# Where the ternary quantization of six weight matrices sits inside the context stage of a fused eight-layer kernel

## The reference, cut to what matters

```
# for each of the 8 context batches: what later attention layers need of the context
k = rms_norm(ctx @ wk_ctx);  v = ctx @ wv_ctx              # layer 1
kv = feature_map(ctx @ Wk)^T (ctx @ Wv)                    # layer 2 (linear attention)
k3, v3 = ctx @ wkv + bkv                                   # layer 3

# for each of six feed-forward weight matrices (gate, up, down of layers 0 and 1)
scale = mean(abs(w)) (+ or max 1e-5)
wq    = clip(round(w / scale), -1, 1) * scale              # so: -1, 0 or +1 times scale
```

## Time and profile before

| | us |
|---|---|
| median of three executions | 2215.29 |
| the profiled execution's own time | 2214.09 |
| its span in the trace | 2212.3 |
| TensorE busy | 2062.1 (93% of the span) |
| VectorE busy | 1121.0 (51%) |
| ScalarE busy | 826.5 (37%) |
| GpSimd busy | 181.4 (8%) |

### The profile page before, as it was taken

One profiled execution on the slowest core, in us unless ns is written; L12 is line 12 of the kernel. 1 busy time (PEld: TensorE's weight loads), 2 busy tenths in 40 slices (PEclk: granted clock), 3 DMA queues, 4 the chain that ended last, 5 costly groups with the idle time before them and its releaser, 6 DMA issues.

```text
span 2212.3 us, 28740 instructions
## 1 busy us (share of the span) xinstructions
PE 2062.1 (93%) x10661; PEld 1168.5 (53%) x10684; DVE 1121.0 (51%) x2469; ACT 826.5 (37%) x1717; POOL 181.4 (8%) x466
## 2 busy tenths in 40 slices
PE   8999999999999798999999999999488888888999
PEld 3444444444666344555555555566244445556665
DVE  1324554258121485555555555487355568774221
ACT  1232233321111264445444455355232235553331
POOL 0011110000000121101110110010100100000000
PEclk9999999999999999999999999999799989998999
DMA  5354442451641511120000011300100502220000
GB/s 227 130 209 174 163 155 103 193 207 60 212 138 59 196 57 42 38 89 21 22 22 22 22 29 40 135 18 10 37 16 15 177 29 88 81 64 10 11 11 15
DMA packets 60315, 185.13 MB, mean 84 GB/s; under 512 B 10578, under 2 KB 29010, under 8 KB 54463
## 3 DMA queue, kind: packets, MB, share of 16 engines
q1 hardware_dynamic: 58451, 145.55, 19.1%
q0 software_dynamic: 1728, 37.75, 4.4%
HBM read 124.61 MB, written 49.50 MB: 79 GB/s over the span
## 4 chain that ended last, share of the span: by engine, by line
PE 71%; DVE 15%; issue 5%; ACT 4%; DMA 2%; POOL 1%; SPq 1%; DVEq 0%; POOLq 0%; ACTq 0%
PE psum L120 47%; PE psum L113 8%; PE psum L1558 5%; PE psum L2612 4%; PE psum L1603 4%; DVE R L654 3%; ACT R L583 2%; DVE small L2491 2%; DVE R L653 1%; PE psum L1146 1%; DVE R L1313 1%; PE psum L2420 1%; DMA d_kv<-WK 1%; DVE R L1312 1%; DVE WK L2497 1%
## 5 line engine op out<-in xcount | busy, mean ns | idle before, releaser
L120 PE MATMUL psum<-R,WK 128*125 128x512 f32 (+10 forms) x3144 | 1084.3, 491 | 34.3 <-DMA WK<-in_ctxT 7.9
L120 PEld LDWEIGHTS psum<-R,WK 128*112 128x112 f32 (+4 forms) x3158 | 516.7, 172 | 545.3 <-issue 421.5
L113 PE MATMUL psum<-small,WK 112*125 112x112 f32 (+5 forms) x2036 | 286.3, 271 | 77.8 <-DVE WK L1303 20.1
L113 PEld LDWEIGHTS psum<-small,WK 112*125 112x125 f32 (+5 forms) x2036 | 225.0, 155 | 185.3 <-issue 76.6
L120 PE MATMUL psum<-WK,R 128*32 128x128 f32 (+5 forms) x1880 | 221.9, 354 | 25.6 <-DMA WK<-d_cd 12.0
L1734 DVE TENSOR_REDUCE small<-psum 112x1 f32<-112x487 f32 x128 | 85.1, 665 | 194.2 <-PE psum L120 190.3
L120 PEld LDWEIGHTS psum<-WK,R 128*32 128x32 f32 (+4 forms) x1880 | 120.2, 135 | 107.7 <-issue 46.8
L1558 PE MATMUL psum<-R,WK 128*112 128x512 f32 x256 | 120.1, 592 | 0.0
L1653 ACT ACTIVATE WK<-psum,small 112x487 f32<-112x487 f32 x128 | 96.9, 757 | 54.2 <-DVE small L1736 53.2
L1603 PE MATMUL psum<-R,WK 125*128 125x448 f32 (+1 forms) x256 | 107.6, 543 | 0.0
L1646 ACT ACTIVATE WK<-WK,small 112x487 f32<-112x487 f32 x128 | 90.0, 703 | 45.8 <-DVE small L1728 45.7
(11 more groups left out here) (237 smaller groups left out, 2137.6 us busy)
## 6 DMA issues: line engine op xcount, KB each, us to landing
R<-in_wf POOLq DMA_DIRECT2D x6, 4096.0 KB, 13.8
d_w<-R POOLq DMA_DIRECT2D x6, 2048.0 KB, 18.1
R<-d_w SPq DMA_DIRECT2D x6, 2048.0 KB, 11.1
WK<-in_ctxT SPq DMA_DIRECT2D x16, 750.0 KB, 6.7
d_v<-WK SPq DMA_DIRECT2D x16, 750.0 KB
R<-in_wq SPq DMA_DIRECT2D x7, 1024.0 KB, 8.0
R<-in_wo SPq DMA_DIRECT2D x6, 1024.0 KB, 15.0
d_k<-X SPq DMA_DIRECT2D x8, 750.0 KB, 5.2
```

The costliest lines, as they stand in the source:

```text
L113: ins = pe.transpose(dst, src, idn[0:k, 0:k])
L120: ins = pe.matmul(dst, lhs, rhs, start=k == 0, stop=k == len(pairs) - 1)
```

## The change

Four edits, all within `context_part`:

- ScalarE takes the four sums of absolute values one at a time, each behind the copy of `k3_0` to `k3_3` (and so ahead of the copy of `T_2`, and of `turn` and `spread` in batches 4 and 5). Each adds one to `context_abs`, and VectorE's sum waits for four of them.
- VectorE makes ternary matrix b no longer at the end of batch b, but behind `v3_0` of batch b + 1 (a function of its own, `ternary`).
- POOL's two transfers go with it: they stand behind the inverse root of sub-tile 0 of batch b + 1.
- SP waits for the last ternary store, and loads the spline inputs, behind the load of context batch 7 instead of ahead of it.

```diff
@@ sync @@
                     sp.dma_start(ctxT[:, b % 2], io.ctxT[:, b]).then_inc(sem(f"context_ctxT{b % 2}"), 16)
+                    if b == 7:
+                        sp.wait_ge(sem("context_ternary"), 6)
+                        sp.wait_ge(sem("ternary_stored"), 16 * 6)
+                        for dst, src in ((table[:, 0], io.table[0]), (table[:, 1], io.table[1]), (points, io.points),
+                                         (knot, io.knot), (way, io.way)):
+                            sp.dma_start(dst, src).then_inc(sem("spline_inputs"), 16)
                     store(sp, b - 1)
...
                     if b == 7:
                         stages[0]["load"](sp)
-                    if b == 6:
-                        sp.wait_ge(sem("context_ternary"), 6)
-                        sp.wait_ge(sem("ternary_stored"), 16 * 6)
-                        for dst, src in ((table[:, 0], io.table[0]), (table[:, 1], io.table[1]), (points, io.points),
-                                         (knot, io.knot), (way, io.way)):
-                            sp.dma_start(dst, src).then_inc(sem("spline_inputs"), 16)
@@ act @@
                         ins.then_inc(act_ring.sem_drained, 1)
+                        if kind == "k3" and b < 6:
+                            if j == 0:
+                                act.wait_ge(sem("context_raw"), 16 * (b + 1))
+                                if b:
+                                    act.wait_ge(sem("ternary_stored"), 16 * b)
+                            act.activation(tern[:, j * 2048:(j + 1) * 2048], raw[:, j * 2048:(j + 1) * 2048], ACT.Abs,
+                                           accum_out=wsum[:, b, j:j + 1]).then_inc(sem("context_abs"), 1)
...
-                    if b < 6:
-                        act.wait_ge(sem("context_raw"), 16 * (b + 1))
-                        if b:
-                            act.wait_ge(sem("ternary_stored"), 16 * b)
-                        for c in range(4):
-                            ins = act.activation(tern[:, c * 2048:(c + 1) * 2048], raw[:, c * 2048:(c + 1) * 2048],
-                                                 ACT.Abs, accum_out=wsum[:, b, c:c + 1])
-                        ins.then_inc(sem("context_abs"), 1)
@@ dve @@
+                        if s == 0 and 1 <= b <= 6:
+                            ternary(dve, link, b - 1)
                         if b == NB - 1:
...
                     if b < 6:
-                        dve.wait_ge(sem("context_abs"), b + 1)
+                        dve.wait_ge(sem("context_abs"), 4 * (b + 1))
...
-                        dve.wait_ge(sem("context_threshold"), b + 1)
-                        for cols in parts:
-                            under = below[:, 0:cols.stop - cols.start]
-                            link(dve.tensor_scalar(under, raw[:, cols], thr[:, b, 1:2], None, ALU.is_lt))
-                            ins = dve.scalar_tensor_tensor(tern[:, cols], raw[:, cols], thr[:, b, 0:1],
-                                                           under, ALU.is_gt, ALU.subtract)
-                            if cols.stop < WF:
-                                link(ins)
-                        ins.then_inc(sem("context_ternary"), 1)
...
+            def ternary(dve, link, w):
+
+                dve.wait_ge(sem("context_threshold"), w + 1)
+                for cols in parts:
+                    under = below[:, 0:cols.stop - cols.start]
+                    link(dve.tensor_scalar(under, raw[:, cols], thr[:, w, 1:2], None, ALU.is_lt))
+                    ins = dve.scalar_tensor_tensor(tern[:, cols], raw[:, cols], thr[:, w, 0:1], under, ALU.is_gt, ALU.subtract)
+                    if cols.stop < WF:
+                        link(ins)
+                ins.then_inc(sem("context_ternary"), 1)
@@ pool @@
                         pool.tensor_tensor(rk, ssp, neghalf[0:SP, :], ALU.pow).then_inc(sem("context_norms"), 1)
+                        if s == 0 and 1 <= b <= 6:
+                            pool.wait_ge(sem("context_ternary"), b)
+                            if b < 6:
+                                pool.dma_start(raw, io.wf[b]).then_inc(sem("context_raw"), 16)
+                            pool.dma_start(d_w[b - 1], tern).then_inc(sem("ternary_stored"), 16)
...
-                        pool.wait_ge(sem("context_ternary"), b + 1)
-                        if b + 1 < 6:
-                            pool.dma_start(raw, io.wf[b + 1]).then_inc(sem("context_raw"), 16)
-                        pool.dma_start(d_w[b], tern).then_inc(sem("ternary_stored"), 16)
```

## The result

| | before | changed | ratio, 95% interval |
|---|---|---|---|
| first comparison, median (executions) | 2212.03 us (7) | 2204.29 us (7) | 0.9957 [0.9943, 0.9971] |
| repeated with the experiments | 2211.43 us (19) | 2204.81 us (12) | 0.9975 [0.9962, 0.9988] |
| profiled execution: own time, span | 2214.09, 2212.3 us | 2204.48, 2202.7 us | |

The change makes the kernel faster, by 0.43% in one comparison and 0.25% in the other; the two intervals overlap only between 0.9962 and 0.9971. The ratios aren't the quotients of the medians; those are 0.9965 and 0.9970, which is 7.7 and 6.6 us. The forecast was 0.9968 as a ratio (2208.3 of 2215.3).

A forecast was written before the change was run, and what follows sets the result against it. TensorE, busy 93% of the span, was taken as the bound, losing time at `T_0` of batches 1 to 6. From 2214.1 us, -21.5 + 10.9 + 3.6 = -7.0 gave 2207.1, or 2208.3 against the median 2215.3; range 2203.5 to 2214.0.

The forecast's parts named there:

- Removal of the stalls, 21.5 us: TensorE's waits at `T_0` of batches 1 to 6, with second waits and slow clock behind them, all go: 21.5 us.
- the second wait of 0.52 us: Right behind each stall at `T_0` of batches 1 to 6, TensorE waits 0.52 us for ScalarE, which needs `kn` too.
- The new stall, 10.9 us: At the ends of batches 0 to 5, the copy of `T_2` stands behind the fourth sum, delaying TensorE: 10.9 us.
- The clock in the stage, two drops of 1.8 us: At two of the six new idle gaps TensorE's clock falls, costing 1.8 us each: 3.6 us, bounds 0 and 10.8.
- The stage's sum: Context stage: -21.5 for the stalls, +10.9 for the new stall, +3.6 for the clock, together -7.0 us.
- Its own time lies 1.2 under the median of 2215.3, against which the forecast is 2208.3: Whole kernel: the profiled execution's 2214.1 us less 7.0 gives 2207.1, restated against the median 2215.3 as 2208.3 us.
- Nothing behind the stage absorbs it: Behind the context stage: attention 0 starts from the last stores, which shift with batch 7, so the -7.0 us stays.
- No drops at all (1): At the new gaps between batches the clock never falls; 2204.7 us, chance 0.14.
- drops at four or more of the six places (2): The clock falls at four to six batch boundaries; 2211.9 to 2215.5 us, no change, chance 0.17.
- The late store (3): The ternary store lands too late for ScalarE's first sum, delaying batches; 2223.8 us at 25 us landing, chance 0.09.
- A stall in sub-tile 1 (4): `kn` of sub-tile 1 comes too late for `T_1`; 2215 us or so, no change, chance 0.05.

The follow-up runs named there:

- the second experiment: Against the changed kernel, only the fourth sum of absolute values moved behind ScalarE's copy of `T_2`; 2192.04 us, ratio 0.9913 to the kernel before.
- The fifth sum: Against the changed kernel, one more sum of absolute values put between the fourth and the copy of `T_2`; 2224.16 us, ratio 1.0057 to the kernel before.
- third experiment: Against the changed kernel, all four sums put back behind the copy of `T_2`, so only the ternary matrix and its transfers moved; 2191.14 us, ratio 0.9908.
- the last experiment: Against the kernel with only the ternary matrix moved, SP's wait for the last ternary store put back ahead of batch 7's load; 2192.57 us, ratio 0.9922.
- the sixth experiment: Against the changed kernel, POOL's two transfers put behind the inverse root of sub-tile 2 instead of 0; 2263.85 us, ratio 1.0244 to the kernel before.

## Why the prediction was right or wrong

**Removal of the stalls, 21.5 us: right.** TensorE no longer waits for `kn`, and in the kernel with the fourth sum behind `T_2` batches 1 to 6 take 389.2 us (75.29 to 464.45), for which 389.4 had been worked out as unstalled. One reading was off, without a part in the sum: the second wait of 0.52 us stands behind five of the six `T_0`, not behind that of batch 1.

**The new stall, 10.9 us: right in place, cause and size.** Forecast 1.8 us at four batch starts and 1.85 in batches 4 and 5. TensorE's waits are 1.82 and 1.96, and the delay is 1.89 at each of the six, which is one sum: from the last context product to the next batch it is 2.86 us (73.82 to 76.68) where the second experiment has 0.97 (266.50 to 267.47), and from `kv` to `spread` 3.19 (338.69 to 341.88) where it has 1.30 (330.03 to 331.33). Six of them are 11.3 us. The forecast was 0.4 short, and the fifth sum took 1.89 more at each.

**The clock in the stage, two drops of 1.8 us: right in the profiled execution.** Batch 1's group of 80 lost 1.7 us. At the end of batch 4, from `spread` to the next batch 3.26 us pass (341.88 to 345.14) instead of 2.62 (331.33 to 333.95), and the group behind takes 35.22 instead of 34.57: 1.3 us together. The repeat had three drops. In the four profiles with idle times of 1.82 us at batch starts (the changed kernel twice, only the sums moved, the transfers late) the clock fell behind 3 of 13 of them, in batch 1, 1 and 4, and behind 4 of the 6 waits of 1.96 us in the first three of these profiles. So the same idle time does not always have the same price. The spread of the executions points the same way, but isn't proof: in the second and third experiment, without idle time at the batch starts, they lie within 2189.3 to 2195.0 and 2189.9 to 2192.4, in the changed kernel's repeat within 2200.4 to 2210.7, and before within 2204.2 to 2216.3; the last experiment, also without such idle time, has one execution at 2199.8 beside five within 2189.9 to 2194.8.

**The stage's sum.** Six batches took 410.9 us before and take 389.2 without stalls, so -21.7; with 11.3 for the new stall, 3.0 for the two drops and -0.6 from the stage's start that is -8.0. Measured: -8.1. The forecast had -7.0 for the same stage; 0.6 of the difference is batch 0's transfers, 0.6 the smaller second drop, and -0.2 and +0.4 the two stalls.

**"Its own time lies 1.2 under the median of 2215.3, against which the forecast is 2208.3": this step failed.** It took the median of three executions as the kernel's level. Over 7 and 19 executions the kernel before lies at 2212.0 and 2211.4, so the term was 3.3 to 3.9 us too high. The gain of 7.0 us was sound: by the medians it is 7.7 and 6.6, by the ratios 9.5 (0.43%) and 5.5 (0.25%). Taken from the measured base, 7.0 us less gives 2205.0 and 2204.4, and the changed kernel takes 2204.3 and 2204.8. The forecast of 2208.3 is only 3.7 us under the kernel before as it was measured over 7 executions, where 7.7 were measured.

The profiled execution, too, was no typical one: with 2214.09 it lies 2.1 and 2.7 us above the two medians. Its rows hold slow groups in batches 1 to 3, 19.13 twice, and this one behind the first stall:

```profile
116.00 19.82 PE L120 MATMUL psum<-R,WK 128*125 128x512 f32 x40
```

Against 17.33 these are 6.1 us, which the prediction took as a fixed part of the 21.5, while it treated the drops of the new kernel as chance. Whether they come in every execution is open, since only this one execution of the kernel before has a trace. Between the two profiled executions the gain is 9.6 us, against the forecast of 7.0: 8.1 in the stage and 1.5 behind it.

**"Nothing behind the stage absorbs it": right on the whole, but the later stages add differences of their own.** Between the two profiled executions the lead is 8.1 us at the end of the stage, 6.6 at 733.44 before (726.85 changed), 9.3 at 1998.92 (1989.65) and 9.6 at the end. The clock plays into it there too. A window of the kernel before, some 15 us ahead of its row at 1998.92:

```profile
1982.00:1986.00 4.00, 4.00 (x23) 2.76 (x22) 1.52 (x3) 1.56 (x5) 0.00 (x0) 0.50 0.00 0
```

The changed kernel's window 9 us earlier, at about the same place of the program:

```profile
1973.00:1977.00 4.00, 4.00 (x44) 2.72 (x43) 2.27 (x6) 3.06 (x12) 0.00 (x0) 1.00 0.01 4
```

Before gets through 23 matmul records at 0.50 in the time of 44 at 1.00. The change edits nothing there; that it is chance is the plain reading, but not shown.

**Rivals.** No drops at all (1) and drops at four or more of the six places (2) did not happen in either profile of the changed kernel. The measured 2204.3 and 2204.8 are rival 1's 2204.7 only by luck: the drops were there, and the base was too high. The late store (3) did not happen, but it was the right thing to watch: the sixth experiment shows its price. A stall in sub-tile 1 (4) did not happen, even with the ternary matrix up to 5 us later.

**The best version.** The change's own sums were better left where they were: with only the ternary matrix moved the kernel takes 2191.1 us, 0.9% under before and 0.6% under the changed kernel, and in context batches 1 to 5 TensorE has no idle time left. The kernel with only the fourth sum moved back is as fast (2192.0).

## What to carry to other kernels

When work is moved on an engine that drains accumulator banks, ask which drain now stands behind it and which product is waiting for that bank; a 1.9 us instruction one place too early cost 13 us over six batches, more than the change gained. Where two edits are made at once, try each alone: here either one removed the stall, and only one of them brought a new one. A forecast in absolute time should rest on more than three executions when these spread as widely as the gain under study: here the kernel before spread over 12 us, and the forecast gain was 7. The profiled execution should be placed among the others before its rows are taken as the kernel's.

## What the runs showed of the hardware that had not been expected

The clock far behind the changed stage can move a time by about half of the change's gain. The last experiment's profiled execution took 2199.84 us, 7.3 above its own median; that of the kernel it is compared with took 2191.14. Two windows of equal length that begin at about the same place of the program; first the last experiment's:

```profile
1964.00:1998.00 34.00, 26.31 (x224) 18.54 (x224) 13.90 (x27) 6.82 (x18) 1.48 (x4) 0.50 0.06 17
```

The window of the kernel with only the ternary matrix moved:

```profile
1960.00:1994.00 34.00, 24.61 (x289) 18.03 (x289) 16.32 (x36) 9.59 (x24) 2.22 (x6) 0.73 0.06 17
```

In the same 34 us TensorE got through 224 matmul records at 0.50 and through 289 at 0.73. Much of that difference lies at the end, where the second kernel has already reached a group of many short records. In time, from the group of six small products in this stretch (1964.63 and 1959.41) to the group of 168 records behind it (1992.39 and 1983.78), the last experiment falls back from 5.2 to 8.6 us, by 3.4. The stretch has gaps between its products in both. Of the 8.7 us between the two spans the changed stage holds 0.8 (530.23 and 529.41 at its end); the rest lies in the stages behind it.

In the kernels with only the ternary matrix moved TensorE also stood once, for 1.14 and 1.42 us, right behind the start of batch 6, waiting for nothing that the profile shows. What it was stays open.
